# ScalarE computes silu, softplus moves to the end of the second scan, scan units from four strips

## The chip, the cores and the metric

The kernel runs on one core of a Trainium2 chip. The metric is the device time of one execution in microseconds (us). Three runs of the kernel before gave 1034.46, 1028.82 and 1028.4, with a median of 1028.82.

## The reference

One layer of a language model tower works on 2 sequences of 2048 tokens with 192 channels. The output is `h + attn(layernorm(h))`, followed by a layer norm and a mixture of experts. Cut to what matters here:

```
zxbcdt = rmsnorm(x) @ in_proj_w
dt  = softplus(zxbcdt[..., -24:] + dt_bias)              # 24 heads
xBC = silu(causal_conv4(zxbcdt[..., 384:896]) + conv_b)  # x 384, B 64, C 64
h   = exp(dt * -exp(A_log)) * h + (dt * x) B             # scan over tokens
y   = (h C + D * x) * silu(z);  h1 = y @ out_proj_w
m   = (silu(v @ w_gate) * (v @ w_up)) @ w_down           # v = rmsnorm(h1)
experts: (silu(x @ w1[e]) * (x @ w3[e])) @ w2[e] * cw[e] # 8 experts and a shared one
cw: sigmoid scores, best 2 of 4 groups, best 2 experts, normed
```

## The kernel before, in words

The 2048 tokens are cut in 16 chunks of 128 tokens, for both sequences at once. The order of the work is written out by hand for each engine, with semaphores between them. A pass of the loop (`body(p, f, b)`) works on three chunks: `p` is prepared (embedding, projections, convolution, steps), `f` is scanned, and `b` goes through the out projection, the MLP (`swiglu`) and the experts. Thirteen passes are the loop, three stand before it and two behind it.

On TensorE (PE) a pass is: out projection of `b`; first scan of `f` (sequence 0); `swiglu` of `b`, six units of two projections and a `down` product; second scan of `f`; input projection of `p`; then nine expert units of `b` with the rest of `p` between them. A projection is split in five fp16 products for precision, all recorded at L1345.

A scan has six units of four heads. In each, PE makes the exponents (L1471), ScalarE (ACT) takes `exp` into `er` (L727), VectorE (DVE) multiplies with the mask into `mr` (L1065), and PE multiplies `mr` by `xd` (L1490) into bank `p_y`. Two heads share one strip of 32 rows of `p_y`, so the four heads 4q to 4q+3 of a unit write two strips. GpSimd (POOL) fills `xw` for the new state (L453).

Silu was made of two steps: ACT takes `tanh(x/2)` and DVE computes `(1+t)x`, which is twice the silu, in `swiglu` (L1107), in the experts (L1230), for `z` (L1010) and for the convolved `x`, `B`, `C` (L1002, L1004). The factors are taken back from the weights by `scale_outputs`. Softplus is `max(x,0) + ln(1+exp(-|x|))`: DVE makes `dx`, `dn`, `am_` (L1018 to L1024) between the experts 0 and 1, ACT takes `exp` and `ln` (L678, L682) at expert 2, POOL then makes the decays. ACT loads a table of functions where the next function isn't in the loaded one (ACT_TABLE_LOAD).

Of the kernel before, what the change touches and what calls it, by code (L numbers as in the profile page):

```python
# [21 lines left out]
ALU = mybir.AluOpType  # L22
# [14 lines left out]
DI = 384  # L37
# [8 lines left out]
HG = 4  # L46
NQ = NH // HG
# [8 lines left out]
HF = NH // 2  # L56
STEP = 1.0 / 16
# [33 lines left out]
def program(nc, tokens, position, vocab_ids, table, weights, norms, conv_w, conv_b, shared_rows, d_skip, w_out, w_down,  # L91
            w2, identity, lower_ones, head_rows, pair_rows, spread_rows, out):
    with ExitStack() as ctx:
# [163 lines left out]
        z_ready = [sem(f"z_ready{i}") for i in range(2)]  # L257
# [41 lines left out]
        weighed, sx_half, gt_half = sem("weighed"), sem("sx_half"), sem("gt_half")  # L299
        halved, decay_p, conv_p, xa_rest_ready = sem("halved"), sem("decay_p"), sem("conv_p"), sem("xa_rest_ready")  # L300
        tap_ready = [sem(f"tap_ready{i}") for i in range(2)]
        xt_tanh, taps_ready = sem("xt_tanh"), sem("taps_ready")
# [101 lines left out]
        def _(pool):  # L404
# [36 lines left out]
            def scan(c, b, after):  # L441
                if later(c):
                    pool.wait_ge(sn_done[b], c)
                for q in range(NQ):
# [5 lines left out]
                    for odd in range(2):  # L450
                        h = slice(q * HG + odd, (q + 1) * HG, 2)
                        o = slice(q * HG * HD, (q + 1) * HG * HD)
                        ins = pool.tensor_tensor(  # L453
                            xw[:, b, o].rearrange("p (g o d) -> p g o d", o=2, d=HD)[:, :, odd, :],
                            xd[:, b, h, odd * HD:(odd + 1) * HD],
                            er[:, r % NER, odd:HG:2, Q - 1:Q].to_broadcast([128, HG // 2, HD]), ALU.mult)
# [83 lines left out]
            def experts(c, p):  # L540

                for e in range(NX):
# [20 lines left out]
            def body(p, f, b):  # L563
# [13 lines left out]
                if p is not None:  # L577
                    convolve(p)
# [9 lines left out]
        def _(act):  # L588
# [59 lines left out]
            def gates(c, i):  # L648
                t = (slice(0, 2), slice(2, KT))[i]
                act.wait_ge(z_done[i], c + 1)  # L650
                if later(c):
                    act.wait_ge(y_ready[1], c)
                act.activation(zs[:, t], (p_y, p_misc)[i][:, 0:(t.stop - t.start) * NB * Q]
                               .rearrange("p (k b t) -> p k b t", b=NB, t=Q), ACT.Tanh, scale=0.5).then_inc(z_ready[i], 1)

            def convolved_out(c):
# [7 lines left out]
                act.activation(xs[:], xa[:], ACT.Tanh, scale=0.5).then_inc(xt_tanh, 1)  # L664
# [84 lines left out]
            def swiglu(c, p):  # L749
                for f in range(NF):  # L750
# [7 lines left out]
                    act.activation(sg[:, f % 2, :], p_pair[f % 2][:, 0:NB * Q], ACT.Tanh, scale=0.5).then_inc(sg_ready, 1)  # L758
# [978 lines left out]
```

## Time and profile before

| | |
|---|---|
| time of the profiled execution | 1034.3 us |
| its span | 1032.5 us |
| PE busy | 863.1 us (84%) |
| PEld busy | 667.5 us (65%) |
| DVE busy | 762.7 us (74%) |
| ACT busy | 553.3 us (54%) |
| POOL busy | 558.4 us (54%) |
| mean granted clock of TensorE | 0.949 |

Busy is the time in which an engine executes an instruction. One execution was profiled; shares are of its span. PEld is the loading of weights, beside PE's products. In the rows below a time of day is counted from the span's start, and one whole pass (515.4 to 575.0) is followed.

### The profile page before, as it was taken

To read this page: it belongs to the slowest core of one execution; us is meant where nothing else is said; L and a number is where in the kernel's file an instruction comes from. 1 tells how busy PE (TensorE), PEld (TensorE's weight loads), DVE (VectorE), ACT (ScalarE), POOL (GpSimd) and SP (SyncE) were. 2 spreads that over 40 slices of the span, in tenths; PEclk is the share of its full clock that TensorE was granted. 3 is DMA by queue.
4 is the path that set the end of the run, shared out by engine and by line. 5 is a ranking of instruction groups with operands and counts; after the bars stand their busy time and mean duration, and the time that the engine had idled before them with its cause. 6 is when DMAs were issued, how large, how long until landed. Compare 5 with 4: busy or idle time off the path is not lost.

```text
span 1032.5 us, 23473 instructions
## 1 busy us (share of the span) xinstructions
PE 863.1 (84%) x7072; PEld 667.5 (65%) x7072; DVE 762.7 (74%) x1821; ACT 553.3 (54%) x1323; POOL 558.4 (54%) x940
## 2 busy tenths in 40 slices
PE   3363989898997988889898988989798998989867
PEld 2232767666776766667666766766676676667746
DVE  5656787868778786877778687777868687786634
ACT  3464465555646464564646456464655556465423
POOL 1453555564655565574556557455555746455513
PEclk9686999899999999999999999999999999999978
DMA  8200000000000000000000000000000000000000
GB/s 221 76 1 12 2 5 16 2 19 0 19 0 4 14 0 19 0 19 0 4 14 1 18 0 19 0 10 9 4 15 0 19 0 15 3 4 10 1 8 9
DMA packets 16469, 15.24 MB, mean 15 GB/s; under 512 B 6322, under 2 KB 15224, under 8 KB 16184
## 3 DMA queue, kind: packets, MB, share of 16 engines
q1 hardware_dynamic: 16440, 14.89, 5.4%
q8 instruction: 14, 0.23, 0.1%
q14 instruction: 15, 0.12, 0.0%
HBM read 10.69 MB, written 4.19 MB: 14 GB/s over the span
## 4 chain that ended last, share of the span: by engine, by line
PE 30%; DVE 24%; issue 23%; POOL 13%; ACT 4%; DMA 4%; SPq 1%; POOLq 1%; DVEq 1%; ACTq 0%
PE bank L1345 14%; POOL w_raw L553 7%; PE bank L1490 5%; DVE mr L1065 4%; DMA tok<-tokens 3%; DVE xa L990 2%; PE bank L1519 2%; DVE sg L1107 2%; POOL r L421 2%; PE bank L1604 2%; PE bank L1555 1%; DVE sg L1230 1%; PE bank L1351 1%; DVE xs L1004 1%; ACT sg L758 1%
## 5 line engine op out<-in xcount | busy, mean ns | idle before, releaser
L453 POOL TENSOR_TENSOR xw<-xd,er 128x32 f32<-128x32 f32 x384 | 141.9, 397 | 99.6 <-ACT er L727 85.8
L553 POOL TENSOR_TENSOR w_raw<-w_raw 128x384 f32<-128x384 f32 x128 | 130.8, 1022 | 102.4 <-ACT w_raw L788 97.0
L1065 DVE SCALAR_TENSOR_TENSOR mr<-er,gm 128x512 f32<-128x512 f32 x192 | 140.9, 767 | 49.6 <-ACT er L727 49.2
L727 ACT ACTIVATE er<-bank 128x512 f32<-128x512 f32 x192 | 110.2, 608 | 52.9 <-PE bank L1471 52.0
L1490 PE MATMUL bank<-mr,xd 128*32 128x128 f32 x1536 | 123.0, 281 | 15.4 <-DVE mr L1065 14.8
L1345 PE MATMUL bank<-x_h,w_hi 128*128 128x256 f16 x288 | 82.7, 287 | 50.0 <-DVE w_raw L1239 49.4
L1604 PE MATMUL bank<-w2t,w_raw 128*128 128x192 f32 x576 | 121.8, 341 | 0.5 <-ACT w_raw L788 0.5
L1490 PEld LDWEIGHTS bank<-mr,xd 128*32 128x32 f32 x1536 | 71.3, 110 | 71.6 <-DVE mr L1065 49.1
L758 ACT ACTIVATE sg<-bank 128x256 f32<-128x256 f32 x96 | 36.8, 383 | 131.0 <-PE bank L1345 131.0
L1604 PEld LDWEIGHTS bank<-w2t,w_raw 128*128 128x128 f32 x576 | 95.4, 200 | 4.2 <-DVE w_raw L1239 1.1
L788 ACT ACTIVATE w_raw<-bank,cw 128x192 f32<-128x192 f32 x256 | 90.6, 430 | 11.5 <-PE bank L1604 9.5
L799 ACT ACTIVATE sg<-bank 128x256 f32<-128x256 f32 x144 | 55.0, 382 | 76.1 <-PE bank L1345 75.7
L1230 DVE SCALAR_TENSOR_TENSOR sg<-sg,bank 128x256 f32<-128x256 f32 x144 | 59.9, 416 | 39.6 <-ACT sg L799 38.5
L1345 PE MATMUL bank<-x_l,w_hi 128*128 128x256 f16 x288 | 82.5, 286 | 0.0
L1345 PE MATMUL bank<-x_h,wt_hi 128*128 128x256 f16 x288 | 82.5, 286 | 0.0
L1345 PE MATMUL bank<-x_h,w_lo 128*128 128x256 f16 x288 | 82.2, 286 | 0.0
L1345 PE MATMUL bank<-x_h,wt_lo 128*128 128x256 f16 x288 | 82.1, 285 | 0.0
L1555 PE MATMUL bank<-wd,gt 128*128 128x192 f32 x384 | 77.3, 331 | 1.3
L990 DVE SCALAR_TENSOR_TENSOR xa<-xr,cw_,xa 128x256 f32<-128x256 f32 x144 | 76.5, 532 | 2.0
L1471 PE MATMUL bank<-ri,lj 128*128 128x512 f16 x192 | 71.9, 388 | 3.4 <-ACT er L727 2.1
L1345 PEld LDWEIGHTS bank<-x_h,w_hi 128*128 128x128 f16 x288 | 29.1, 101 | 65.3 <-DVE w_raw L1239 62.3
L532 POOL TENSOR_TENSOR xa<-xa,taps 128x256 f32<-128x256 f32 x48 | 36.6, 763 | 55.7 <-ACT taps L645 53.2
(228 smaller groups left out, 2286.1 us busy)
## 6 DMA issues: line engine op xcount, KB each, us to landing
out<-w_raw SPq DMA_DIRECT2D x16, 192.0 KB, 2.0
w_raw<-weights SPq DMA_DIRECT2D x1, 1924.0 KB, 8.9
wt_raw<-weights SPq DMA_DIRECT2D x2, 962.0 KB, 14.6
pos<-position SPq DMA_DIRECT2D x16, 96.0 KB, 3.0
tok<-tokens SPq DMA_DIRECT2D x16, 70.0 KB
sums<-lj SPq DMA_DIRECT2D x16, 64.0 KB, 2.2
ri<-sums SPq DMA_DIRECT2D x64, 12.0 KB
w2t<-w SPq DMA_DIRECT2D x1, 864.0 KB, 19.3
```

Of the source, the lines that this page charges most:

```text
L453: ins = pool.tensor_tensor(xw[:, b, o].rearrange("p (g o d) -> p g o d", o=2, d=HD)[:, :, odd, :], xd[:, b, h, odd * HD:(odd + 1) * HD], e ...
L553: pool.tensor_tensor(acc[:], acc[:], wt_out[:, e % NWT], ALU.add).then_inc(acc_done, 1)
L727: act.activation(er[:, r % NER], p_d[r % 2][:].rearrange("p (h i) -> p h i", h=HG), ACT.Exp)\
L788: ins = act.activation(wt_out[:, e % NWT, b], p[:, b * D:(b + 1) * D], ACT.Copy, scale=cw[:, b, e - 1:e])
L990: ve.scalar_tensor_tensor(xa[:, m], xr[:, m, :, k:k + Q], cw_[:, m, k:k + 1], xa[:, m], ALU.mult, ALU.add)\
L1065: ve.scalar_tensor_tensor(mr[:, r % NER], er[:, r % NER], 1.0, gm[:, b, :].unsqueeze(1).to_broadcast([128, HG, Q]), ALU.min, ALU.mult)\
L1230: ve.scalar_tensor_tensor(sg[:, e % 2, :], sg[:, e % 2, :], 1.0, p_pair[e % 2][:, 0:NB * Q], ALU.add, ALU.mult).then_inc(sx_half, 1)
L1345: ins = pe.matmul(out_, a, b, start=(i == 0), stop=(i == len(parts) - 1))
L1471: pe.matmul(p_d[r % 2][:], lj[:, b, f, :], ri[:, b, f, g * HG:(g + 1) * HG, :].rearrange("p h i -> p (h i)"), start=True, stop=True).then_ ...
L1490: ins = pe.matmul(p_y[row:row + 32, k * Q:(k + 1) * Q], xd[:, b, h, :], mr[:, r % NER, h % HG, :], start=(h % 2 == 0), stop=(h % 2 == 1))
L1555: ins = pe.matmul(p_out[0][:, b * D:(b + 1) * D], gt[:, f, b * Q:(b + 1) * Q], wd[:, f, :], start=(f == 0 and b == 0), stop=(f == NF - 1), ...
L1604: ins = pe.matmul(p_out[(e + 1) % 2][:, b * D:(b + 1) * D], hh[:, e % NHH, b * Q:(b + 1) * Q], w2t[:, e, :], start=True, stop=True)
```

## The change

ACT computes silu directly (`ACT.Silu`) in all four places, and DVE's `(1+t)x`, `scale_outputs` and the factor on `dsk` go. The small projection for `dt` moves on PE from the middle of the `z` projection to the second scan, DVE's `dx`, `dn`, `am_` move to the fifth unit of that scan, ACT's `exp` and `ln` to its end and POOL's decays behind it. PE's `running_sums` moves from expert 4 to 2, the `operands` one expert ahead. The heads of a scan unit are chosen anew, so that four of the six units write all four strips of `p_y`; for these, POOL's `xw` is one instruction in place of two.

```diff
+UNITS = ((0, 2, 4, 6), (1, 3, 5, 7), (8, 10, 9, 11), (12, 14, 13, 15), (16, 18, 20, 22), (17, 19, 21, 23))
...
@@ gpsimd scan
-                    for odd in range(2):
-                        h = slice(q * HG + odd, (q + 1) * HG, 2)
+                    heads, step = unit_heads(q)
+                    for odd in ((heads[0] % 2,) if step == 2 else (0, 1)):
+                        of = slice(0, HG) if step == 2 else slice(odd, HG, 2)
...
@@ gpsimd body
                 if p is not None:
+                    if b is not None:
+                        steps_decay(p)
                     convolve(p)
...
@@ scalar: z, x B C, swiglu, experts
-                               .rearrange("p (k b t) -> p k b t", b=NB, t=Q), ACT.Tanh, scale=0.5).then_inc(z_ready[i], 1)
+                               .rearrange("p (k b t) -> p k b t", b=NB, t=Q), ACT.Silu).then_inc(zs_ready[i], 1)
...
-                act.activation(xs[:], xa[:], ACT.Tanh, scale=0.5).then_inc(xt_tanh, 1)
+                act.activation(bc[NS:128], xa[0:NS, KT], ACT.Silu).then_inc(b_ready, 1)
+                act.activation(xs[:], xa[:], ACT.Silu).then_inc(xs_ready, 1)
...
-                    act.activation(sg[:, f % 2, :], p_pair[f % 2][:, 0:NB * Q], ACT.Tanh, scale=0.5).then_inc(sg_ready, 1)
+                    act.activation(sg[:, f % 2, :], p_pair[f % 2][:, 0:NB * Q], ACT.Silu).then_inc(sg_ready, 1)
...
-                    act.activation(sg[:, e % 2, :], p_pair[e % 2][:, 0:NB * Q], ACT.Tanh, scale=0.5).then_inc(sx_ready, 1)
+                    act.activation(sg[:, e % 2, :], p_pair[e % 2][:, 0:NB * Q], ACT.Silu).then_inc(sx_ready, 1)
...
@@ scalar body
                 if b is not None:
+                    if p is not None:
+                        softplus(p)
                     split_x(b)
...
@@ vector swiglu, experts
-                    ve.scalar_tensor_tensor(sg[:, t % 2, :], sg[:, t % 2, :], 1.0, p_pair[t % 2][:, 0:NB * Q],
-                                            ALU.add, ALU.mult).then_inc(gt_half, 1)
...
-                    if e == 1 and p is not None:
-                        steps_dt(p)
...
@@ vector body
-                    scan(f, 1, {} if b is None else {1: lambda: norm2(b), 3: lambda: norm2_apply(b)})
+                    scan(f, 1, {} if b is None else {1: lambda: norm2(b), 3: lambda: norm2_apply(b),
+                                                     4: lambda: None if p is None else steps_dt(p)})
...
@@ tensor scan, body
-                    for h in range(q * HG, (q + 1) * HG):
+                    heads, _ = unit_heads(q)
+                    for h in UNITS[q]:
...
+                def tokens_steps_and_turn():
+                    if p is not None:
+                        project_dt(p, b)
+                    turn_x(b)
```

Below, a name in brackets behind "waits" is the semaphore that the instruction is held for; a wait that stands on an earlier row holds all that follow on the engine.

ACT, the start of `swiglu` in the loop, of before and then of the change:

```order
L751 REGISTER_ALU
L757 REGISTER_ALU [waits gu_done]
L758 ACTIVATE sg<-bank 128x256 [waits hh_ready]
L751 REGISTER_ALU
L758 ACTIVATE sg<-bank 128x256 [waits hh_ready,gu_done]
```

```order
L758 REGISTER_ALU
L764 REGISTER_ALU [waits gu_done]
L765 ACT_TABLE_LOAD
L765 ACTIVATE sg<-bank 128x256 [waits hh_ready]
L758 REGISTER_ALU
L765 ACTIVATE sg<-bank 128x256 [waits hh_ready,gu_done]
```

A table load has come in, behind the wait for PE's first products.

ACT, from the end of the second scan to the first expert, of the change (before, `er` was followed at once by `x_h`, and there was no load in the stretch):

```order
L734 ACTIVATE er<-bank 128x512 [waits xw_ready,m_ready,d_done]
L685 ACTIVATE de<-dn 128x48 [waits dl_ready,dn_ready]
L689 ACT_TABLE_LOAD [waits pab_ready]
L689 ACTIVATE dl<-de 128x48 [waits de_ready]
L624 CAST x_h<-bank 128x256 [waits h13_done,xnt_done]
L625 CAST x_h<-bank 64x256
L634 COPY xr<-bank 128x4x128 [waits xa_rest_ready,halo_kept,xa_ready,x_done0]
L642 ACTIVATE xa<-xr,cb_,cw_ 128x256 [waits xs_ready,b_ready,xr_ready0]
```

```order
L642 ACTIVATE xa<-xr,cb_,cw_ 128x256
L801 REGISTER_ALU
L806 ACT_TABLE_LOAD [waits gt_ready]
L806 ACTIVATE sg<-bank 128x256 [waits h13_done]
L774 ACTIVATE th<-bank 128x16 [waits cw_ready,router_done]
```

Softplus with one load stands ahead of `x_h` now, and one more load ahead of the first expert's `sg`, before the wait for PE.

ACT, the end of the experts and the start of the scan, of the change:

```order
L795 ACTIVATE w_raw<-bank,cw 128x192
L713 ACT_TABLE_LOAD [waits s_decayed1]
L713 ACTIVATE eend<-bank 128x48 [waits lj_ready]
L719 ACTIVATE ecx<-bank 128x512 [waits t1_ready1,cumx_done0]
L719 ACTIVATE ecx<-bank 128x256 [waits t1_ready1,cumx_done1]
L795 ACTIVATE w_raw<-bank,cw 128x192 [waits acc_done,ex_done]
```

The load ahead of `eend` is new here, and so is one between the last `sg` of `swiglu` and the first `er` of the second scan. In all, a pass of the loop has five loads now, and had two.

## Rows read from the trace of the kernel before

**Rows 1.** Busy time by stretch of one pass (PE, PEld, DVE, ACT, POOL, clock)
```profile
515.40:525.60 10.20, 9.24 (x79) 5.80 (x78) 6.81 (x11) 6.76 (x18) 9.30 (x18) 1.00 0.13 36
525.60:536.00 10.40, 10.16 (x86) 8.88 (x85) 8.00 (x21) 2.93 (x8) 2.83 (x5) 1.00 0.00 0
536.00:547.30 11.30, 10.89 (x99) 7.33 (x97) 8.57 (x19) 5.80 (x13) 8.13 (x17) 1.00 0.00 0
547.30:575.00 27.70, 23.10 (x191) 19.79 (x190) 22.87 (x61) 18.39 (x48) 14.62 (x21) 0.94 0.02 4
```

**Rows 2.** Timeline of PE, experts (start, us, what; idle before in brackets)
```profile
556.26 0.40 PE L1345 MATMUL bank<-x_h,w_hi 128*128 128x256 f16 x1 [2.81 <-DVE w_raw L1239]
561.95 0.28 PE L1345 MATMUL bank<-x_h,w_hi 128*128 128x256 f16 x1 [0.28 <-DVE w_raw L1239]
568.84 0.84 PE L1421 MATMUL bank<-idf,xs 128*128 128x128 f32 x6 [1.44 <-DVE xs L1004]
```

**Rows 3.** Busy time by us, columns as in rows 1: the clock's fall
```profile
555.00:556.00 1.00, 0.00 (x0) 0.00 (x0) 0.96 (x4) 0.63 (x2) 0.26 (x1) 0.93 0.00 0
557.00:558.00 1.00, 1.00 (x7) 0.69 (x6) 1.00 (x4) 0.98 (x2) 0.71 (x1) 0.50 0.00 0
```

**Rows 4.** Groups of instructions by line, DVE (busy, mean ns, idle before)
```profile
L1230 DVE SCALAR_TENSOR_TENSOR sg<-sg,bank 128x256 f32<-128x256 f32 x144 | 59.9, 416 | 39.6 <-ACT sg L799 38.5
L1004 DVE SCALAR_TENSOR_TENSOR xs<-xs,xa 128x1024 f32<-128x1024 f32 x16 | 29.1, 1819 | 0.6
L1010 DVE SCALAR_TENSOR_TENSOR zs<-zs,bank 128x256 f32<-128x256 f32 (+1 forms) x32 | 17.3, 545 | 0.0
L1021 DVE SCALAR_TENSOR_TENSOR dn<-dx 128x48 f32<-128x48 f32 x16 | 10.4, 650 | 0.5
```

**Rows 5.** Timeline of ACT around a table load
```profile
555.35 0.24 ACT L678 ACTIVATE de<-dn 128x48 f32<-128x48 f32 x1 [1.39 <-DVE dn L1021]
555.61 1.28 ACT L682 ACT_TABLE_LOAD   x1
556.91 0.24 ACT L682 ACTIVATE dl<-de 128x48 f32<-128x48 f32 x1
```

**Rows 6.** Timeline of ACT and of PE, end of the experts
```profile
515.45 1.15 ACT L727 ACTIVATE er<-bank 128x512 f32<-128x512 f32 x2
...
515.06 2.22 PE L1531 MATMUL bank<-wo,y 128*128 128x192 f32 x12
```

**Rows 7.** Timeline of PE, one unit of the second scan
```profile
538.14 0.64 PE L1490 MATMUL bank<-mr,xd 128*32 128x128 f32 x8
538.71 0.39 PE L1471 MATMUL bank<-ri,lj 128*128 128x512 f16 x1
```

**Rows 8.** Timeline of DVE, first scan
```profile
521.91 0.35 DVE L946 TENSOR_SCALAR onehot<-tok,ids 70x256 bf16<-70x256 int32 x1 [0.45 <-DMA tok<-tokens]
```

**Rows 9.** Timeline of ACT and of PE, swiglu
```profile
526.96 0.38 ACT L758 ACTIVATE sg<-bank 128x256 f32<-128x256 f32 x1 [2.01 <-PE bank L1345]
...
532.22 0.28 PE L1345 MATMUL bank<-v_h,w_hi 128*128 128x256 f16 x1 [0.24 <-DVE gt L1113]
```

**Rows 10.** Timeline of ACT, DVE and PE, second scan
```profile
536.01 1.08 ACT L727 ACTIVATE er<-bank 128x512 f32<-128x512 f32 x2
...
536.94 1.38 DVE L1065 SCALAR_TENSOR_TENSOR mr<-er,gm 128x512 f32<-128x512 f32 x2
...
544.38 0.28 PE L1345 MATMUL bank<-u_h,w_hi 128*128 128x256 f16 x1
```

**Rows 11.** Timeline of DVE, the first experts
```profile
550.02 0.42 DVE L1239 TENSOR_TENSOR w_raw<-sg,bank 128x256 f32<-128x256 f32 x1
554.32 0.20 DVE L1018 TENSOR_TENSOR dx<-bank,shared 128x48 f32<-128x48 f32 x1
555.78 0.42 DVE L1239 TENSOR_TENSOR w_raw<-sg,bank 128x256 f32<-128x256 f32 x1
561.48 0.42 DVE L1239 TENSOR_TENSOR w_raw<-sg,bank 128x256 f32<-128x256 f32 x1
```

More of the change, by code:

```diff
@@ L46 @@
 HG = 4
+DT_AT = 64
 NQ = NH // HG
@@ L56, with unit_heads @@
 HF = NH // 2
+UNITS = ((0, 2, 4, 6), (1, 3, 5, 7), (8, 10, 9, 11), (12, 14, 13, 15), (16, 18, 20, 22), (17, 19, 21, 23))
+assert sorted(h for unit in UNITS for h in unit) == list(range(NH)) and len(UNITS) == NQ
+def unit_heads(q):
+    heads = sorted(UNITS[q])
+    step = heads[1] - heads[0]
+    return heads, step
 STEP = 1.0 / 16
@@ L812, in experts @@
                             gates(p, 0)
-                        if e == 2:
-                            softplus(p)
+                        if e == 3:
+                            operands(p)
                         if e == 4:
-                            operands(p)
                             convolved_out(p)
@@ L857, in body @@
                     softplus(p)
-                    if f is not None:
-                        scale_outputs()
                     operands(p)
@@ L889, in setup_first @@
                 ve.wait_ge(in_small, 16 * N_SMALL)
-                ve.tensor_scalar(dsk[:], dsk[:], 4.0, None, ALU.mult).then_inc(setup_v, 1)
-                ve.wait_ge(setup_v, setup_steps.next(0))
                 ve.wait_ge(setup_p, SETUP_P)
@@ L1377, in project_in_x @@
                     pe.wait_ge(w_in_lo, 2)
+                pe.wait_ge(u_hi_ready, c + 1)
+                pe.wait_ge(u_hi_tail, c + 1)
+                pe.wait_ge(u_lo_ready, c + 1)
+                pe.wait_ge(u_lo_tail, c + 1)
+                if later(c):
+                    pe.wait_ge(dx_ready, c)
+                if b is not None:
+                    pe.wait_ge(h1_ready, b + 1)
+                settle(pe)
+                for i in range(NB):
+                    ins = split_products(p_out[0][:, DT_AT + i * NH:DT_AT + (i + 1) * NH], slice(DI, ZD), u_h, u_l,
+                                         slice(i * Q, (i + 1) * Q), False)
+                ins.then_inc(dt_done, 1)
+            def project_in_x(c):
                 pe.wait_ge(u_hi_ready, c + 1)
@@ L1403, in project_in_z @@
                     if k == 2:
-                        for b in range(NB):
-                            ins = split_products(p_misc[:, 256 + b * NH:256 + (b + 1) * NH], slice(DI, ZD), u_h, u_l,
-                                                 slice(b * Q, (b + 1) * Q), False)
                         ins.then_inc(z_done[1], 1)
@@ L1647, in body @@
                     pre_turn(p)
+                def tokens_steps_and_turn():
+                    if p is not None:
+                        project_dt(p, b)
+                    turn_x(b)
                 if f is not None:
-                    scan(f, 1, {} if b is None else {3: lambda: turn_x(b)}, p)
+                    scan(f, 1, {} if b is None else {3: tokens_steps_and_turn}, p)
                 elif b is not None:
```

79 lines of the change are left out of this document (27 added, 52 removed).

## The prediction

> **What bounds the kernel now.** I read the busy times by stretch first. A pass of the loop takes 59.6 us (515.4 to 575.0), and fourteen of the sixteen chunks are prepared in such passes. In `swiglu` TensorE is busy 10.16 of 10.40 us and in the scans 9.24 of 10.20 and 10.89 of 11.30, so little waiting can be won there; among the experts it is 23.10 of 27.70, and VectorE 22.87 [rows 1]. The reader should see that the experts are the one stretch with room. The timeline of TensorE says what the room is: 2.81 us before expert 3, waiting for the second `hh` product, 0.28 before expert 5, and 1.44 before the transposes of `xs`, all three ended by VectorE [rows 2]. The first one costs more than itself: after 2.1 us of it the granted clock falls to 0.50, that is from 2.4 to 1.2 GHz, and stays there in the next stretch [rows 3]. TensorE then works at half speed until shortly before 559.2. Next I read what VectorE and ScalarE do there by groups and by time, and how a table load stands in ScalarE's row.
>
> **What the change gives.** On VectorE nine `sg` steps of 416 ns, one `xs` of 1819 and two `zs` of 545 go from the experts of each pass, 6.7 us [rows 4]; `dx`, `dn`, `am_` move away from between the experts 0 and 1, where they take 554.32 to about 555.4, 1.0 us of which `dn` is 0.65 [rows 4, 11]. Only what stands on the way to the three waits of TensorE counts. That ScalarE computes `xs` at its end costs it nothing new: the tanh did as many elements. The time of a Silu against a Tanh no row shows; the tanh of `swiglu` takes 0.38 us [rows 9], I take the same, and bound it by that and by twice that, which would be hidden in ScalarE's idle time in most places.
>
> **What it costs.** ScalarE switches tables five times a pass and not twice. A load takes 1.28 us, and from the start of the load to the next instruction are 1.30 us (555.61 to 556.91) [rows 5]; the usual overlap of 0.1 is lost as well, so 1.4 us where ScalarE is on the path. Place by place, as a shift of the work against the pass shown:
>
> A. Ahead of `eend`, at the end of the experts. ScalarE has no idle time there, and `er` starts at 515.45, TensorE's out projection at 515.06, both behind ScalarE's last two weightings [rows 6]. All 1.4 us are on the path. **+1.4.**
>
> B. First scan and `swiglu`. A unit of a scan keeps TensorE from 538.14 to 538.71, 0.57 us, on two strips [rows 7]. On four strips it is between 0.57 (nothing) and half of it, 0.29; I take 0.36, since the filling at its start doesn't halve. Two of the four such units lie behind VectorE's wait for the tokens' DMA at 521.91 [rows 8], which ends at the same time whatever is faster before it; so 0.4 us are won. POOL's merged `xw` falls under the same wait and is costed at nothing; with the wait gone, it would win up to 0.4. In `swiglu` the load stands behind the wait for TensorE (`gu_done`), so ScalarE's 2.01 us of idle time before `sg` at 526.96 do not hide it [rows 9]. The first `gt` comes 1.3 later by the load and 0.4 earlier without VectorE's step; with the 0.4 of the strips the third unit starts 0.4 later than now. A wait of 0.24 us at 532.22 [rows 9] goes, and the rest is caught up since VectorE has become fast enough everywhere else in the stretch. **0.0** at its end.
>
> C. Second scan. The load stands between the last `sg` of `swiglu` and `er`, which now starts at 536.01; it will at 537.4, and `mr`, now at 536.94, at 538.05 [rows 10]. VectorE is busy nearly throughout this scan, so the 1.1 us stay. `dx`, `dn`, `am_` add 1.0 before the last unit. Against it stand 0.2 of strips and 0.3 of a wait for `xn` that shrinks. TensorE's input projection, now at 544.38 [rows 10], starts 1.6 later: **+1.6.** Softplus ahead of `x_h` (`de`, load, `ln`: 1.8 us) delays `x_l` to about 548.2, but TensorE asks for it only after its projection, at about 548.9; that cover is 0.7 us thick. The moved small `dt` products, ten of some 0.03 us, fall into a wait for `xn`.
>
> D. First experts. ScalarE copies and scales the projection (3.3 us), then loads (+1.3), then computes `sg`; without VectorE's step the first `hh` is at 550.02 + 1.6 + 1.3 − 0.4, less 0.2 of slack, that is 552.3. From there 4.3 us of routing (550.02 to 554.32), no steps of softplus and no `sg` step: the second `hh` at 556.6 where it is at 555.78 now [rows 11]. Expert 3 starts 0.8 later, after an idle time of 1.95 and not 2.81, because all that TensorE does before it has moved by 1.6 too. For the fourth `hh`, now at 561.48 [rows 11], two more `sg` steps and half of the `zs` fall away: 561.1, and expert 5 starts **0.4 earlier** than its 561.95 [rows 2]. If the clock falls all the same, TensorE itself is the bound and expert 5 starts **0.3 later**. `running_sums` is then in time that is idle anyway or saves 0.3, counted in this.
>
> E. The transposes. ScalarE has `xs` at about 564, before TensorE asks; the 1.44 us of wait go [rows 2], and 0.2 of the tail of a product with it: **−1.6**, which makes −2.0 or −1.3 for the pass up to here.
>
> **The sum.** A stands in the next pass, so a pass changes by +1.4 − 2.0 = −0.6 with the clock kept, and by +1.4 − 1.3 = +0.1 with the clock lost. TensorE's idle time of 1.95 us lies just under the 2.1 after which the clock fell; I take half of the passes each, −0.25, times 14: −3.5. The first two chunks, where ScalarE waits and VectorE is the bound, lose `zs`, `xs` and `sg` steps (3 us of [rows 4] in each) and pay one or two loads: −3 together. The two last passes save a step of 0.42 at four places where TensorE waits: −1.6. Sum −8. The profiled execution took 1034.3 us, 1.8 more than its span of 1032.5, and 5.5 more than the median of the runs; −8 makes 1026 of it, and of the median 1028.8 it makes **1021 us**.
>
> **What the skill says.** The Trainium skill, page "ScalarE: Activation LUTs", section "What ACT_TABLE_LOAD costs", gives each switch about 1.38 us of drain on top of the load, 2.66 us in all; this trace disagrees, since the next instruction starts 1.30 us after the load [rows 5]. The same page's section "Table sets: the hidden batching unit" says to do all functions of one set before switching, and this change does the opposite.
>
> **The rivals.**
>
> 1. *Second clock loss* (slower). C puts 1.25 us of idle time on TensorE before the last unit of the second scan, and 0.4 at its start. If that is enough for the clock to fall there too, the input projection and the experts 0 to 2, which are TensorE's own bound, run at half speed for a while: the stretch that follows now (556.3 to 559.2) costs 1.45 us of work, and here, with nothing to hide it, 1.5 to 2. [...] A pass is then +0.1 + 1.7, times 14 = +25, less 4.6 at the ends: **1049 us**. For it: VectorE is full there. Against it: between its waits TensorE works, and idle times of 1.44 us do not lower the clock now [rows 2]. Chance 0.18.
>
> 2. *The clock is kept everywhere* (faster). The idle time before expert 3 falls below what the clock bears in every pass, and the merged `xw` and the strips win 0.5 in the first scan, because the tokens' DMA comes in time. A pass is −1.1, times 14 = −15.4, less 4.6: **1009 us**. For it: 1.95 is less than 2.1. Against it: the wait for the DMA follows POOL's last sum of the pass before, which moves with A. Chance 0.26.
>
> 3. *Nothing is hidden after a load.* If each load held ScalarE as long again before its next instruction, A, B, C and D would pay 1.3 us more each, 5.2 a pass, 73 in all: **1094 us**. By the rule on the drain named above it would go this way. Rows 5 speak against it. Chance 0.03.
>
> 4. *The load of C or D is covered* by work that I take to be on the path, or Silu is dearer than Tanh. Both stay within the range of the forecast; chance 0.03 for more than that, on either side.
>
> **Chances and range.** The forecast has 0.50, with a range of its own of 1012 to 1031. About 10 us, 1%, are what a measurement of this kernel tells from no change: 1018.5 to 1039. Of the forecast 0.17 lies below 1018.5 and 0.33 within; rival 2 is all faster; rival 1 is 0.03 within and 0.15 slower; rival 3 slower. That makes faster 0.44, same 0.37, slower 0.19. The range reaches from below rival 2 to short of rival 1's far end: 1002 to 1046.
>
> **What would show it.** In the profile after: five loads a pass, 84 in all; VectorE's busy time down by some 9 us a pass; `er` of the second scan 1.3 us behind the last `sg`; out projection 1.4 us later behind the last expert; no wait before the transposes; a scan unit of four strips in 0.36 us; the idle time before expert 3 at 1.95 us, and the mean clock above 0.949. The forecast is wrong if the wait before expert 3 is as long as now, if a new wait of over 0.5 us stands before the router's products (the cover of C gone), or if the clock falls in the second scan.

## The result

The changed kernel took 1048.2 us (median of four runs, 1043.8 to 1052.1), the kernel before 1031.6 (1028.4 to 1034.5): a ratio of 1.0168 with an interval of 1.0141 to 1.0194. It is 1.7% slower. The forecast of 1021 was wrong in sign and in size, and the time lies outside the range of 1002 to 1046. (The fourth run of the kernel before lifted its median from 1028.8, on which the forecast stood, to 1031.6; that is 2.8 of the 27 us.) The profiled execution took 1049.2 us, its span 1047.3. Engine busy times of that execution:

```profile
PE 844.0 (81%) x7072; PEld 651.3 (62%) x7072; DVE 632.7 (60%) x1516; ACT 621.1 (59%) x1387; POOL 506.9 (48%) x812
```

VectorE does 130 us less than before (762.7 to 632.7, 8.1 a pass of the sixteen), close to the 9 that was expected. So the work did go. It did not come back as time, and the next question is at which landmark of a pass it was lost. I took the same landmarks from both traces, as offsets from the start of the out projection, and of twelve passes the median (`hh` is the product of an expert's two projections, written by VectorE as `w_raw<-sg,bank`):

| from the out projection (us) | before | after | change | forecast |
|---|---|---|---|---|
| input projection | 29.30 | 31.16 | +1.86 | +1.6 |
| first `hh` | 34.95 | 37.48 | +2.53 | +2.3 |
| second `hh` | 40.70 | 42.86 | +2.16 | +0.8 |
| transposes of `xs` | 53.78 | 53.75 | 0.0 | −1.3 (clock lost) to −2.0 |
| next out projection | 59.34 | 60.71 | +1.37 | +0.1 to −0.6 |

The table places the fault in one row: between the first and the second `hh`. The stretches ahead of it and behind it came out within 0.3 us.

**Places A and C (table loads).** ScalarE's timeline in the changed kernel, at the end of the experts and at the start of the second scan; these answer to [rows 6] and [rows 10]:

```profile
516.14 0.73 ACT L795 ACTIVATE w_raw<-bank,cw 128x192 f32<-128x192 f32 x2 [0.27 <-PE bank L1592]
516.89 1.28 ACT L713 ACT_TABLE_LOAD   x1
518.19 0.21 ACT L713 ACTIVATE eend<-bank 128x48 f32<-128x48 f32 x1
...
520.25 1.13 ACT L734 ACTIVATE er<-bank 128x512 f32<-128x512 f32 x2
...
540.67 0.38 ACT L765 ACTIVATE sg<-bank 128x256 f32<-128x256 f32 x1 [0.98 <-PE bank L1315]
541.07 1.28 ACT L734 ACT_TABLE_LOAD   x1
542.37 1.68 ACT L734 ACTIVATE er<-bank 128x512 f32<-128x512 f32 x3
```

From the last two weightings to `er` it is 4.11 us, and was 2.66: +1.45. Each load holds ScalarE for 1.28 us, and the next instruction starts 1.30 after it, at 518.19 and at 542.37. There are five loads a pass, as the groups by line show (columns: busy, mean ns; idle before):

```profile
L689 ACT ACT_TABLE_LOAD x16 | 20.5, 1283 | 0.3
L713 ACT ACT_TABLE_LOAD x16 | 20.5, 1283 | 0.3
L765 ACT ACT_TABLE_LOAD x15 | 19.2, 1283 | 30.7 <-PE bank L1315 30.7
L734 ACT ACT_TABLE_LOAD x15 | 19.2, 1283 | 0.3
L806 ACT ACT_TABLE_LOAD x15 | 19.2, 1283 | 0.3
```

**TensorE**, timeline of a pass; [rows 2] and [rows 7] are what stood there before:

```profile
502.47 0.28 PE L1315 MATMUL bank<-x_h,w_hi 128*128 128x256 f16 x1 [3.06 <-DVE w_raw L1216]
...
512.88 0.82 PE L1403 MATMUL bank<-idf,xs 128*128 128x128 f32 x6
...
519.83 2.22 PE L1517 MATMUL bank<-wo,y 128*128 128x192 f32 x12 [0.23 <-ACT w_raw L795]
...
522.60 0.43 PE L1475 MATMUL bank<-mr,xd 128*32 128x128 f32 x8 [0.34 <-DVE mr L1052]
522.96 0.39 PE L1455 MATMUL bank<-ri,lj 128*128 128x512 f16 x1
```

The wait before the transposes (1.44) is gone, a unit on four strips takes 0.36 us, both as forecast. The wait before expert 3 is 3.06 us; before it was 2.81, and the forecast had 1.95. The granted clock behind it (columns as in [rows 3]):

```profile
502.00:503.00 1.00, 0.53 (x5) 0.49 (x6) 1.00 (x4) 0.00 (x0) 0.00 (x0) 1.00 0.00 0
...
504.00:505.00 1.00, 1.00 (x5) 0.93 (x4) 1.00 (x5) 0.93 (x3) 0.00 (x0) 0.50 0.00 0
```

It falls from 2.4 to 1.2 GHz again, for 3.4 us. It does so at this wait in 11 of the 14 passes (10 before). From 120 to 960 us I count 47.8 us at the lower level, and 37.5 before; the mean over the span is 0.944, and was 0.949.

**What VectorE did in that stretch.** Its timeline from the first `hh` to the second; it answers to [rows 11]:

```profile
496.62 0.42 DVE L1216 TENSOR_TENSOR w_raw<-sg,bank 128x256 f32<-128x256 f32 x1 [1.11 <-ACT sg L806]
...
497.73 0.48 DVE L994 SCALAR_TENSOR_TENSOR xa<-xr,cw_,xa 128x256 f32<-128x256 f32 x1
498.12 0.72 DVE L1150 TENSOR_TENSOR g_ge<-g_ge,shared 128x32 f32<-128x32 f32 x1
498.77 0.18 DVE L1151 TENSOR_TENSOR g_gt<-gs 128x32 f32<-128x32 f32 x1
498.87 1.01 DVE L994 SCALAR_TENSOR_TENSOR xa<-xr,cw_,xa 128x256 f32<-128x256 f32 x1
499.80 0.70 DVE L1157 TENSOR_TENSOR g_gt<-g_gt,g_ge 128x32 f32<-128x32 f32 x1
500.43 1.26 DVE L994 SCALAR_TENSOR_TENSOR xa<-xr,cw_,xa 128x256 f32<-128x256 f32 x1
...
501.99 0.42 DVE L1216 TENSOR_TENSOR w_raw<-sg,bank 128x256 f32<-128x256 f32 x1
```

No instruction behind the first one waits for anything, yet instructions of one form and shape take 0.48, 1.01 and 1.26 us (`xa`), and comparisons of 128x32 elements take 0.18 and then 0.70 (`g_gt`). The slow ones lie in one interval, 498.1 to 501.7. GpSimd's timeline of the same time:

```profile
497.93 2.53 POOL L545 TENSOR_TENSOR xa<-xa,taps 128x256 f32<-128x256 f32 x3 [0.58 <-ACT taps L651]
500.42 0.99 POOL L563 TENSOR_TENSOR w_raw<-w_raw,h 128x384 f32<-128x384 f32 x1
```

GpSimd adds the products of ScalarE's taps to the convolution (`convolve`), and right behind it sums expert 0: from 497.93 to 501.41 without a gap. These are the slow microseconds of VectorE. Each slow instruction ends just behind one of GpSimd: `g_ge` at 498.84 where GpSimd's first `xa` ends at 498.80, `xa` at 499.88 (499.60), `g_gt` at 500.51 (500.46), the last `xa` at 501.69 (501.41). That GpSimd's work slows them is the theory to test. Its rival is that the loads and the clock alone ate the gain. The yardstick is the stretch from the first to the second `hh`, median over the fourteen passes: 5.75 us before, 5.37 after.

### The profile page after: what moved, and what is told of

Its sections match the earlier page's. It is cut to its first block, busy times and chain, and to the rows that moved or that the text cites. A ratio compares the mean times of both kernels' runs of the same rounds, so it can differ in the third digit from the quotient of the medians.

```text
span 1047.3 us, 23150 instructions
## 1 busy us (share of the span) xinstructions
PE 844.0 (81%) x7072; PEld 651.3 (62%) x7072; DVE 632.7 (60%) x1516; ACT 621.1 (59%) x1387; POOL 506.9 (48%) x812
## 4 chain that ended last, share of the span: by engine, by line
issue 31%; PE 26%; POOL 21%; DVE 9%; ACT 6%; DMA 4%; POOLq 1%; SPq 1%; ACTq 0%; DVEq 0%
PE bank L1315 13%; POOL w_raw L566 8%; DMA tok<-tokens 4%; DVE mr L1052 3%; PE bank L1541 3%; PE bank L1475 2%; POOL xa L545 2%; POOL xw L466 2%; PE bank L1592 2%; PE bank L1504 1%; POOL state L479 1%; POOL w_raw L563 1%; PE bank L1455 1%; POOL t L484 1%; ACT er L734 1%
## 5 line engine op out<-in xcount | busy, mean ns | idle before, releaser
L566 POOL TENSOR_TENSOR w_raw<-w_raw 128x384 f32<-128x384 f32 x128 | 128.3, 1002 | 183.5 <-ACT w_raw L795 176.2
L1052 DVE SCALAR_TENSOR_TENSOR mr<-er,gm 128x512 f32<-128x512 f32 x192 | 147.1, 794 | 100.8 <-ACT er L734 100.7
L466 POOL TENSOR_TENSOR xw<-xd,er 128x64 f32<-128x64 f32 (+1 forms) x256 | 114.9, 472 | 131.1 <-ACT er L734 116.5
L1475 PE MATMUL bank<-mr,xd 128*32 128x128 f32 x1536 | 97.3, 289 | 52.6 <-DVE mr L1052 50.4
L1216 DVE TENSOR_TENSOR w_raw<-sg,bank 128x256 f32<-128x256 f32 x144 | 60.2, 420 | 104.8 <-ACT sg L806 103.8
L1475 PEld LDWEIGHTS bank<-mr,xd 128*32 128x32 f32 x1536 | 44.5, 110 | 110.7 <-DVE mr L1052 100.0
L1455 PE MATMUL bank<-ri,lj 128*128 128x512 f16 x192 | 74.2, 397 | 26.7 <-ACT ecx L719 17.9
L994 DVE SCALAR_TENSOR_TENSOR xa<-xr,cw_,xa 128x256 f32<-128x256 f32 x144 | 90.1, 627 | 2.3 <-ACT xa L642 0.4
L1097 DVE TENSOR_TENSOR gt<-sg,bank 128x256 f32<-128x256 f32 x96 | 39.2, 419 | 60.1 <-ACT sg L765 60.1
L1541 PE MATMUL bank<-wd,gt 128*128 128x192 f32 x384 | 73.0, 326 | 0.0
```

Source lines behind the costliest of these rows:

```text
L466: ins = pool.tensor_tensor(xw[:, b].rearrange("p (g o d) -> p g o d", o=2, d=HD)[:, first // 2:first // 2 + n, odd, :], xd[:, b, h, odd * ...
L566: pool.tensor_tensor(acc[:], acc[:], wt_out[:, e % NWT], ALU.add).then_inc(acc_done, 1)
L994: ve.scalar_tensor_tensor(xa[:, m], xr[:, m, :, k:k + Q], cw_[:, m, k:k + 1], xa[:, m], ALU.mult, ALU.add)\
L1052: ve.scalar_tensor_tensor(mr[:, r % NER], er[:, r % NER], 1.0, gm[:, b, :].unsqueeze(1).to_broadcast([128, HG, Q]), ALU.min, ALU.mult)\
L1216: ve.tensor_tensor(hh[:, e % NHH, :], sg[:, e % 2, :], p_pair[e % 2][:, NB * Q:2 * NB * Q], ALU.mult)\
L1455: pe.matmul(p_d[r % 2][:].rearrange("p (h i) -> p h i", h=HG), lj[:, b, f, :], ri[:, b, f, of, :], start=True, stop=True).then_inc(d_done, 1)
```

## The experiments

Each ratio is to the kernel before, which ran beside it (its medians were 1028.7 to 1032.5 us, so differences in us between experiments hold to some 4 us).

**1. Without the loads.** At all places where ScalarE has the silu, the tanh alone; nothing takes the place of VectorE's step, so this kernel leaves out the factor `x` of every silu and serves for timing only.

```diff
-ACT.Silu
+ACT.Tanh, scale=0.5
```

> The changed kernel with Tanh (scale 0.5) in all places of Silu and nothing in place of VectorE's (1+t)x: the factor x is left out of every silu. Everything else stands as in the changed kernel, but a pass has two table loads and not five. Theory 1 (GpSimd's convolution now lies under VectorE's routing and slows it): the loads ahead of eend, swiglu and the second scan go, 3.0 us of a pass (61.1 to about 58), some 1005 us in all, and the stretch from the first to the second hh stays at 5.3 us or more. Theory 2 (the loads alone, there is no slowing beside them): the same time or a little less, and that stretch is back at the 4.3 us that the prediction had.

Measured: 995.2 us, ratio 0.9648 (0.9607 to 0.9688). TensorE's one wait for an `hh` in the pass shown, and a VectorE group:

```profile
537.76 0.28 PE L1315 MATMUL bank<-x_h,w_hi 128*128 128x256 f16 x1 [3.03 <-DVE w_raw L1216]
```
```profile
L1157 DVE TENSOR_TENSOR g_gt<-g_gt,g_ge 128x32 f32<-128x32 f32 x16 | 10.3, 641 | 0.1
```

The three extra loads of a pass (84 in the run, and 33 here) cost 53 us in all (I had expected 43), 3.4 a pass by the means of the twelve passes. Silu itself costs nothing more than the tanh: the experts' `sg` takes 385 ns in both kernels, `xs` 1057. The stretch between the `hh` takes 5.32 us, as in the changed kernel, with the wait of 3.03 and with `g_gt` at 641 ns. So the loads are the larger price of the change; they are not what made VectorE slow.

**2. The convolution later.** GpSimd's `convolve` moves from ahead of the experts to behind the sum of expert 0, and waits there for the fourth `hh`, when the routing is over.

```diff
                     if p is not None:
+                        if e == 0:
+                            pool.wait_ge(hh_ready, c * NX + 4)
+                            convolve(p)
                         if e == 4:
...
-                    convolve(p)
+                    else:
+                        convolve(p)
```

> The changed kernel with GpSimd's convolution (and with it the sum of expert 0 ahead of it) held back until the fourth hh. Theory 1: VectorE's taps take 0.53 us again and not 0.63 on average, the first to the second hh takes 4.3 to 4.6 us and not 5.4, the wait before expert 3 falls to about 2, a pass gets 0.8 to 1.1 us shorter, 1033 to 1037 us. Theory 2: nothing changes within 3 us, or it gets slower because xs waits for the convolution.

Measured: 1040.0 us, ratio 1.0078 (1.0041 to 1.0115), 8 us better than the change. The stretch fell from 5.37 to 2.96 us (expected: 4.3 to 4.6). TensorE's timeline, waits among the experts of one pass:

```profile
503.04 0.28 PE L1319 MATMUL bank<-x_h,w_hi 128*128 128x256 f16 x1 [0.22 <-DVE w_raw L1220]
...
506.17 0.28 PE L1319 MATMUL bank<-x_h,w_hi 128*128 128x256 f16 x1 [1.21 <-DVE w_raw L1220]
...
512.94 0.28 PE L1319 MATMUL bank<-x_h,w_hi 128*128 128x256 f16 x1 [1.05 <-DVE w_raw L1220]
```

The wait of 3.06 is now 0.22, and 23.9 us are spent at the lower clock and not 47.8. In its place stand 1.21 and 1.05. The last one is new: ScalarE's silu of `xs` follows at expert 4 and now waits for the late convolution, and behind it in ScalarE's queue stands the `sg` of the next expert. In 7 of the 14 passes the clock now falls in the second scan, at a wait of 1.53 us.

**3. The same, and the silu of `xs` one expert later.**

```diff
-                        if e == 4:
+                        if e == 5:
                             convolved_out(p)
```

> The changed kernel with GpSimd's convolution held back until the fourth hh, and ScalarE's silu of x, B, C one expert later, so that it does not wait for it. The earlier run with the first edit alone won 8 us and got two new waits of TensorE, 1.21 and 1.05 us before later experts. Theory 1: the second of them goes, a pass gets 1.0 shorter still, 1025 to 1030 us. Rival: TensorE has no room there and waits as long before the transposes, 1040 us.

Measured: 1010.9 us, ratio 0.9815 (0.9774 to 0.9856), so 37 us better than the change and well below the 1025 to 1030 expected, with a mean clock of 0.974 and no stretch at the lower level from 120 to 960 us. VectorE's and GpSimd's timelines, same place of the pass as above:

```profile
540.67 0.42 DVE L1220 TENSOR_TENSOR w_raw<-sg,bank 128x256 f32<-128x256 f32 x1 [1.11 <-ACT sg L810]
...
542.37 0.48 DVE L998 SCALAR_TENSOR_TENSOR xa<-xr,cw_,xa 128x256 f32<-128x256 f32 x1
542.76 0.18 DVE L1161 TENSOR_TENSOR g_gt<-g_gt,g_ge 128x32 f32<-128x32 f32 x1
542.88 0.48 DVE L998 SCALAR_TENSOR_TENSOR xa<-xr,cw_,xa 128x256 f32<-128x256 f32 x1
...
543.66 0.42 DVE L1220 TENSOR_TENSOR w_raw<-sg,bank 128x256 f32<-128x256 f32 x1
544.00 1.08 DVE L1149 TENSOR_TENSOR e_ge<-sv 128x128 f32<-128x128 f32 x1
```
```profile
543.93 0.99 POOL L563 TENSOR_TENSOR w_raw<-w_raw,h 128x384 f32<-128x384 f32 x1 [2.54 <-ACT w_raw L794]
...
549.35 0.73 POOL L545 TENSOR_TENSOR xa<-xa,taps 128x256 f32<-128x256 f32 x1 [4.42 <-DVE w_raw L1220]
```

The same instructions, with GpSimd idle: `xa` 0.48 and 0.48, `g_gt` 0.18, 3.0 us from `hh` to `hh`. The difference of 2.4 us to the changed kernel is thus what GpSimd's work costs under the routing. Not all of it is won: the sum of expert 0 (`w_raw<-w_raw,h`, 543.93) now lies behind the second `hh`, where the first `e_ge` takes 1.08 us and not the 0.28 of the changed kernel (502.33), and the stretch to the third `hh` grew from 2.33 to 3.13. So 1.6 us a pass are won on VectorE up to the third `hh`. The gain of 37 us is 2.6 a pass. The other 1.0 goes along with TensorE's clock, which fell in 12 of the 14 passes of the changed kernel and in none here; no run separates the two.

**4. The convolution under the experts instead.** As 3, but released by the second `hh`, where VectorE is also full.

```diff
-                            pool.wait_ge(hh_ready, c * NX + 4)
+                            pool.wait_ge(hh_ready, c * NX + 2)
```

> The changed kernel with GpSimd's convolution released at the second hh and not at the fourth, so that it lies under VectorE's ranks of the experts; silu of x, B, C one expert later as in the version with 1010.9 us. Theory 1 (GpSimd's work slows VectorE's wherever both run at once): the first to the second hh takes 3.0 us, but the second to the third 4 us or more and not 3.1, and of the 37 us at least 10 are lost again: 1020 to 1035. Rival (it was the place in GpSimd's queue, or the start of the experts alone): as fast as with the fourth hh, 1008 to 1014.

Measured: 1056.3 us, ratio 1.0252 (1.022 to 1.0285), slower than expected. The first stretch is 2.96 us as in 3, the one from the second to the third `hh` 4.65 (3.13 in 3). VectorE and, below, GpSimd:

```profile
507.08 0.42 DVE L1220 TENSOR_TENSOR w_raw<-sg,bank 128x256 f32<-128x256 f32 x1
507.42 1.06 DVE L1149 TENSOR_TENSOR e_ge<-sv 128x128 f32<-128x128 f32 x1
508.40 0.94 DVE L998 SCALAR_TENSOR_TENSOR xa<-xr,cw_,xa 128x256 f32<-128x256 f32 x1
509.27 0.81 DVE L1154 TENSOR_TENSOR e_ge<-e_ge,shared 128x128 f32<-128x128 f32 x1
...
511.66 0.41 DVE L1220 TENSOR_TENSOR w_raw<-sg,bank 128x256 f32<-128x256 f32 x1
```
```profile
507.34 0.99 POOL L563 TENSOR_TENSOR w_raw<-w_raw,h 128x384 f32<-128x384 f32 x1 [2.12 <-ACT w_raw L794]
508.29 2.57 POOL L545 TENSOR_TENSOR xa<-xa,taps 128x256 f32<-128x256 f32 x3
```

The first `e_ge` (1.06) is slow in experiment 3 too, beside the sum of expert 0. What the convolution adds are the three behind it: `xa` 0.94 twice and `e_ge` 0.81, where experiment 3 has 0.47, 0.47 and 0.28, together the 1.5 us by which the stretch is longer. The slowness moves with GpSimd's convolution, which shows the cause and not only a cure. From the first to the third `hh` this kernel takes 7.61 us, the changed one 7.70, experiment 3 6.13. TensorE's long wait moved along: 2.65 to 2.81 us before expert 4, behind which the clock fell in 11 of the 14 passes. From 120 to 960 us the lower level lasted 51.2 us, against none in experiment 3. The 1.5 us of the stretch make 21 of the 45 us between the two; the clock is the likely source of the rest.

**5. The old units.** The changed kernel with the scan units of four consecutive heads.

```diff
-UNITS = ((0, 2, 4, 6), (1, 3, 5, 7), (8, 10, 9, 11), (12, 14, 13, 15), (16, 18, 20, 22), (17, 19, 21, 23))
+UNITS = tuple(tuple(range(4 * q, 4 * q + 4)) for q in range(6))
```

> The changed kernel with units of four heads in a row, as before, so each writes two strips. Prediction: a unit takes TensorE 0.57 us and not 0.36, and 0.4 us of it count in the first scan, 0.2 in the second: 4 to 9 us slower, 1052 to 1057. Rival: VectorE and the tokens' DMA bound the scans, nothing within 3 us.

Measured: 1044.5 us, ratio 1.015 (1.0124 to 1.0176), against 1.0168 with the strips. The groups of the unit's products, first of the changed kernel, then of this one:

```profile
L1475 PE MATMUL bank<-mr,xd 128*32 128x128 f32 x1536 | 97.3, 289 | 52.6 <-DVE mr L1052 50.4
```
```profile
L1475 PE MATMUL bank<-mr,xd 128*32 128x128 f32 x1536 | 124.1, 282 | 29.5 <-DVE mr L1052 28.9
```

The strips save TensorE 26.8 us of busy time, and 21.5 of these turn into longer waits for VectorE's `mr`. My expectation of a loss without them was a miss: TensorE waits for `mr` in the scans, and the strips shorten only what waits.

**6. Silu in the experts and for `xs` and `zs`, the tanh in `swiglu`.** VectorE's step comes back there, with the half in `wd` (`ACT.Copy`, scale 0.5, once); three loads a pass and not five.

```diff
-                    act.activation(sg[:, f % 2, :], p_pair[f % 2][:, 0:NB * Q], ACT.Silu).then_inc(sg_ready, 1)
+                    act.activation(sg[:, f % 2, :], p_pair[f % 2][:, 0:NB * Q], ACT.Tanh, scale=0.5).then_inc(sg_ready, 1)
...
+                    ve.scalar_tensor_tensor(sg[:, t % 2, :], sg[:, t % 2, :], 1.0, p_pair[t % 2][:, 0:NB * Q],
+                                            ALU.add, ALU.mult).then_inc(gt_half, 1)
```

> The changed kernel, but swiglu keeps tanh and VectorE's (1+t)x (and w_down its factor 0.5); so a pass has three table loads, and those in swiglu and ahead of the second scan go. Theory 1: they give back 1.6 us (1.4 of the second scan, 0.2 of swiglu), less 0.3 for VectorE's step; a pass of 59.7, about 1029 us, with the wait before expert 3 still near 3 us. Theory 2: that wait goes back to 2 us too, because it comes of ScalarE's delay: a pass of 58.7, about 1015 us.

Measured: 1030.7 us, ratio 1.0015 (0.998 to 1.005), as expected, but loosely: its ten runs lie between 1020.9 and 1038.0. It is 17.5 us better than the change by the medians and 16 by the ratios; that is what the two loads around `swiglu` cost. In the profiled run the `swiglu` ends on TensorE at the same place of a pass as in the changed kernel (22.72 and 22.75 us behind the out projection), and `er` of the second scan starts at 20.74 and not 22.53, the input projection at 29.69 and not 31.16. So it is the load of place C that costs, and VectorE's six steps in `swiglu` cost nothing visible. The stretch between the `hh` stays at 5.35.

**7. This hybrid with the convolution late** (edits of 2, 3 and 6 together).

> The hybrid (tanh in swiglu, Silu elsewhere, three table loads; measured at 1030.7) with GpSimd's convolution held back and the silu of x, B, C one expert later. Theory 1: the two gains add up, 1.0 to 1.5 us a pass, 1010 to 1017 us, faster than the kernel before. Theory 2: 1030 as without.

Measured: 994.6 us, ratio 0.9643 (0.9622 to 0.9664), 3.6% faster than the kernel before, 54 us better than the changed one and better than expected.

The convolution's place is worth 36 us here and 37 in experiment 3; the two loads 17.5 in 6 and 16.3 here (1010.9 to 994.6). The two causes add up, and this is the fastest version here that computes the layer.

**8. The same with the old units** (edit of 5 on 7).

> The best version so far (hybrid, convolution held back, 994.6 us) with units of four heads in a row, two strips each. If strips count once the experts no longer wait: 4 to 9 us slower, 999 to 1004. If VectorE bounds the scans, as in the first test of this: the same within 3 us.

Measured: 994.9 us, ratio 0.9664 (0.9648 to 0.968), 0.2% apart from 7. TensorE's waits for `mr` (sum us, count, longest), of 7 and of this one:

```profile
PE bank L1485 <- DVE mr L1059: 37.3, 61, 1.2
```
```profile
PE bank L1485 <- DVE mr L1059: 20.1, 54, 1.1
```

So the strips show no worth even where the rest is cured.

**9. The kernel before, with only the convolution late.** There ScalarE's tanh of `xs` moves to expert 5 and VectorE's step to expert 6.

```diff
                             steps_decay(p)
+                            pool.wait_ge(hh_ready, c * NX + 4)
+                            convolve(p)
...
+                        if e == 5:
                             convolved_out(p)
...
+                        if e == 6:
                             convolved(p)
```

> The kernel before with GpSimd's convolution held back in the same way (tanh of x, B, C and VectorE's step on it one expert later each). Theory 1: the routing was slowed before already, by 1.4 us of 5.75; first to second hh 4.3 and the wait before expert 3 from 2.8 to 1.4 us, the clock kept more often: 1.0 to 1.5 us a pass, 1010 to 1017 us. But xs is later by up to 2 us, which may bring the wait of 1.44 before the transposes to over 2 and leave 1025. Theory 2: no change.

Measured: 1040.7 us, ratio 1.0075 (1.0049 to 1.0101): no gain, a miss. The stretch fell from 5.75 to 3.78, so the mechanism is the same there. What took it back are TensorE's waits, sums over the run:

```profile
PE bank L1349 <- DVE w_raw L1242: 48.9, 49, 1.9
PE bank L1425 <- DVE xs L1007: 47.1, 16, 6.1
```

Those before the transposes grew by 16 us (31.2 before), and those for `hh` did not shrink (49.4 before) but came in more pieces. The wait before the transposes is now 2.57 us in every pass (1.44 before), and the clock, which no longer fell behind the wait before expert 3, fell behind this one in 8 of the 14 passes; from the transposes to the next out projection a pass takes 7.1 us and not 5.6. With VectorE's 1.8 us step for `xs` still behind the convolution, the later place is not free.

**10. The kernel before with the softplus moved and the strips, its tanh kept.** TensorE's `running_sums` stay at expert 4. Against the kernel before, the two places on VectorE's side and the units (the softplus of the other engines moves as in the change):

```diff
-                    scan(f, 1, {} if b is None else {1: lambda: norm2(b), 3: lambda: norm2_apply(b)})
+                    scan(f, 1, {} if b is None else {1: lambda: norm2(b), 3: lambda: norm2_apply(b),
+                                                     4: lambda: None if p is None else steps_dt(p)})
...
+UNITS = ((0, 2, 4, 6), (1, 3, 5, 7), (8, 10, 9, 11), (12, 14, 13, 15), (16, 18, 20, 22), (17, 19, 21, 23))
```

> The kernel before with the softplus at the end of the second scan and the four-strip units, but with tanh and VectorE's (1+t)x kept: two table loads a pass. Theory 1 (convolution and the sum of expert 0 now lie under the routing): VectorE saves the 1.07 us of dx, dn, am_ between the experts 0 and 1 and loses 1.0 to GpSimd again, and softplus delays the second scan by 1.0; a pass is 59.6 to 60.6, 1030 to 1045 us. Theory 2 (loads alone are to blame): all that is left of the change is gain, below 1020 us.

Measured: 1063.1 us, ratio 1.0306 (1.0283 to 1.0328), slower than any theory gave. TensorE before expert 3, and one VectorE group:

```profile
565.76 0.28 PE L1354 MATMUL bank<-x_h,w_hi 128*128 128x256 f16 x1 [3.76 <-DVE w_raw L1247]
```
```profile
L1184 DVE TENSOR_TENSOR g_gt<-g_gt,g_ge 128x32 f32<-128x32 f32 x16 | 14.0, 877 | 0.1
```

The wait is 3.76, with `g_gt` at 877 ns, but the stretch between the `hh` is 5.7 us, as before. The loss stands mostly ahead of it: the first `hh` comes 36.44 us behind the out projection and not 34.94, of which 0.35 is the second scan, longer by `dx`, `dn`, `am_`, and the rest comes behind ScalarE's softplus and the second load, which now stands between the convolution's copies and the first `sg` (`sg` 1.75 later). Another 0.6 comes before the transposes, and 64.9 us are spent at the lower clock and not 37.5. So this part of the change alone costs 31 us, and with the silu and the rest of the change it is 15 less (1063.1 to 1048.2).

**11. The same with the convolution late.** Here too `xs` and VectorE's step for it go one expert later.

> Tanh kept, softplus at the end of the second scan, four-strip units (measured at 1063), now with GpSimd's convolution held back until the fourth hh and ScalarE's and VectorE's steps on x, B, C one expert later. Theory 1: the slowing goes as in the changed kernel (37 us there), less what the later xs costs before the transposes: 1030 to 1042 us. Rival: with tanh it is the second scan, longer by VectorE's softplus steps, that costs the 31 us, and nothing is won.

Measured: 1062.2 us, ratio 1.0321 (1.0295 to 1.0347), again a miss. TensorE's timeline, the waits before expert 3 and before the transposes:

```profile
508.43 0.28 PE L1360 MATMUL bank<-x_h,w_hi 128*128 128x256 f16 x1 [1.43 <-DVE w_raw L1252]
...
522.33 0.93 PE L1448 MATMUL bank<-idf,xs 128*128 128x128 f32 x6 [2.58 <-DVE xs L1020]
```

The 3.76 fell to 1.43, and the wait before the transposes grew from 1.43 to 2.58. Behind the latter the clock fell in 10 of the 14 passes, and in four passes it fell in the second scan. With experiment 9 it says that the later convolution pays, in these kernels, only where ScalarE computes the silu and VectorE has no step behind it.

## Why the prediction was wrong

**Step D failed, in the sentence "From there 4.3 us of routing (550.02 to 554.32)".** I read the routing's duration from the trace of before as if it were its own, and let it follow 1.5 us later unchanged. It was not its own. In the trace of before it already lay beside GpSimd's convolution (550.60 to 553.03), and the 0.65 us of `dn` [rows 4], which I booked as work that goes, lay beside the sum of expert 0 (554.25 to 555.26). In the changed kernel `dn`, in its new place, takes 0.255, and on the way to the second `hh` everything takes 5.37 us and not 4.3. With GpSimd idle there it takes 3.0 (experiment 3). So the 4.3 were about 3.0 of work and 1.3 of slowing; 0.4 more of slowing lay on `dn`, which left its place. The trace of before had it for everyone to read: `gs` took 0.58 us there (at 550.77), `xa` 0.95 (551.49), `g_ge` 0.71 (552.37), where experiment 3 has 0.17, 0.48 and 0.18, together 1.4 less. The changed kernel has 2.4. The rows give the split: `g_ge`, the second `xa` and `g_gt` are 1.6 us longer beside the convolution (1.4 before), and the last `xa`, which ends behind the sum of expert 0, 0.8. That sum used to fall on `dn`; it now follows the convolution without a gap and falls on the routing. Experiment 3 has it alone, on `e_ge`, at the same 0.8 (1.08 against 0.28).

**What it made of the sum.** The second `hh` came at +2.16 and not +0.8, of which 1.1 are this step and 0.25 what C and the first `hh` missed. The wait before expert 3 was then 3.06, and the clock fell behind it in 11 of 14 passes, where I had half of them. A pass became +1.37 by the median of twelve and +1.31 by the mean of all fourteen, and the forecast had −0.25. Fourteen times the mean is +18.3, the ends gave back 3.5 (the forecast: 4.6), and the sum of +15 is the difference of the spans (1032.5 to 1047.3). Of the 23 us between this and the −8 of the forecast, about 17 are the later second `hh` in passes that I had at +0.1, 5 are the half of the passes that I gave the kept clock, and 1 the ends.

The bound of 2.1 us that I gave the clock was a misreading as well. [Rows 3] put the fall at about 555.9, 2.4 us into the wait, and no one length of a wait decides it: the clock held through the same wait of 2.81 in four passes of before, and it fell at a wait of 1.53 us in seven passes of experiment 2.

**A** was right: +1.4 forecast, 1.45 measured at `er`, 1.4 at the out projection. **B** was near: its end is 0.2 late, and the four-strip unit takes 0.36; but that the strips are worth anything (0.4 there, 0.2 in C) is not borne out by experiments 5 and 8. **C** was right within 0.3 us, and its load is the one of the two around `swiglu` that costs (experiment 6). That Silu takes as long as the tanh, which I assumed, holds (experiment 1). **E** was right in its wait: the wait of 1.44 is gone, `xs` is in time.

**The rivals.** Rival 3 (nothing is hidden after a load) fell with 1.30 us from load to next instruction. Rival 1, the second clock loss, came true in one of fourteen passes: at 674.0, in the second scan, and the first `hh` of that pass came 39.24 us behind the out projection and not 37.48, 1.8 late (the forecast priced it at 1.7). One more fall stands in the first scan of the next pass (714.9), and once, from 622.8, the lower clock lasted 6.8 us. These three passes take 62.2 to 62.5 us; they lift the mean of the twelve passes 0.3 above the median (0.2 before). Rival 2, the clock kept everywhere, did not happen in the changed kernel, but it did in all fourteen passes of experiment 3, whose wait before expert 3 is 0.7 us, at a mean clock of 0.974 and 1010.9 us. That this is near the rival's 1009 is luck: the rival had the idle time at 1.95 us and knew nothing of the convolution. What was missing among the rivals is one in which the duration of VectorE's routing itself grows.

**Where the gain went.** The time that VectorE gained among the experts was real: from the second `hh` to the transposes a pass is 2.19 us shorter. The loads and the moved steps put the first `hh` 2.5 us later and the next out projection 1.4 later again. GpSimd's slowing of the routing kept more from being won, at the one wait that also costs the clock.

The Trainium skill, page "SBUF — State Buffer", section "SBUF: two separate sides", says that VectorE and GpSimd take a pair of ports under an exclusive lock, and that the one which comes second is blocked until the other's instruction is done; on VectorE's side it names, among others, instructions with two inputs from SBUF, against a GpSimd instruction that reads SBUF. The traces agree: `g_gt<-g_gt,g_ge` goes from 185 ns (experiment 3) to 641 as a mean, and a slow instruction ends just behind one of GpSimd. `w_raw<-sg,bank`, which has only `sg` in SBUF (`bank` is TensorE's result in PSUM), is not slowed: 44 of its 144 executions in the changed kernel lie wholly beside GpSimd's work and take 422 ns on average, the other 100 take 420. `e_ge<-sv` (1.06 and 1.08 us in experiments 4 and 3) is a comparison of two views of `sv`, so it has two inputs as well, though the row shows one name. So has `g_gt<-gs`, which stays at 180 ns; in the pass shown it starts at 498.77, as one GpSimd instruction ends (498.80), and the next starts at 498.87. An instruction with one input can be longer too: `am_<-dx` takes 0.31 us in its new place and 0.17 in the old, and no run tells why. Whether the block is the ports' or another one no run here separates; that it comes with GpSimd's work, experiments 3 and 4 show.

## What to carry to other kernels

A duration read from a trace holds what the other engines did at that moment. Before a step is moved or counted as removed, compare its rows with rows of the same form and shape elsewhere in the trace (here 0.48 against 0.95 us, 0.18 against 0.71), and ask whom its slowness will fall on when it is gone. Ask the same of a wait that costs the clock: moved elsewhere, it can cost the clock there (experiments 2, 4 and 9). A strip, a table load or a removed step is worth what the wait behind it allows; price the load at the place where ScalarE is the last to come, and mix the two ways (silu here, tanh there), so that a switch is paid only where VectorE's time is needed.

## What the runs showed of the hardware

- VectorE's small instructions grow 2.6- to 3.8-fold beside GpSimd's elementwise ones: `g_gt` 128x32 0.18 to 0.64 us (mean of 16), `xa` 128x256 0.48 to 1.26, `e_ge` 128x128 0.28 to 1.06. They end just behind GpSimd's instruction. Taken together 3.5 us of GpSimd work cost VectorE 2.4 us. `w_raw<-sg,bank`, with one input in PSUM, keeps its 0.42.
- Eight products with 128x32 weights took 0.36 us on four strips and 0.57 on two, so not half; the mean of one is 289 and 281 ns.
- A table load took 1283 ns as the mean of every group of the 84, and the next instruction started 1.30 us after its start. In experiment 1, 51 loads fewer were worth 53 us; in experiment 6, 30 fewer were worth 16 to 17.5. Silu and tanh take the same time (385 ns for 128x256, 1057 for 128x1024).
- The granted clock went to 0.50 at TensorE's wait of 3.06 us in 11 of 14 passes (2.81 us before: 10 of 14), at one of 2.57 in 8 of 14 (experiment 9), at one of 1.53 in 7 of 14 (experiment 2); in experiment 3, whose longest wait for an `hh` is 1.25 us, in none of the 14.
